# Softplus polynomial of a Mamba branch, from Horner steps to quadratic factors with ScalarE squares

## The reference

```python
x = x + _L0_attn_ref(_layernorm(x, axis=-1), ...)
x = x + _L0_xattn_ref(ctx_1024, _layernorm(x, axis=-1), ...)
x = x + _L0_ffn_ref(_layernorm(x, axis=-1), ...)

def _L0_xattn_ref(hidden_states, z, ...):
    ...
    x = silu(xc + conv_b[None, :, None])
    x_dbl = jnp.einsum('bdl,ed->bel', x, x_proj_w)
    dt_low, Bm, Cm = jnp.split(x_dbl, [dt_rank, dt_rank + d_state], axis=1)
    dt = jnp.einsum('brl,dr->bdl', dt_low, dt_proj_w)
    dt = jax.nn.softplus(dt + dt_proj_b[None, :, None])
    A = -jnp.exp(A_log)
    def step(state, inp):
        d, b, c, u = inp
        dA = jnp.exp(d[..., None] * A)
        state = state * dA + (d * u)[..., None] * b[:, None, :]
        y = jnp.einsum('bdn,bn->bd', state, c)
        return (state, y)
    ...
```

## Time and profile before

| | us |
|---|---|
| median of 3 runs | 1650.46 |
| lowest and highest | 1649.22, 1653.79 |
| the profiled execution, its own time | 1649.75 |
| the span that its trace covers | 1647.9 |
| PE busy | 1406.0 (85%) |
| VectorE busy | 1218.4 (74%) |
| ScalarE busy | 604.9 (37%) |

### The profile page before, as it was taken

One profiled execution on the slowest core, in us unless ns is written; L12 is line 12 of the kernel. 1 busy time (PEld: TensorE's weight loads), 2 busy tenths in 40 slices (PEclk: granted clock), 3 DMA queues, 4 the chain that ended last, 5 costly groups with the idle time before them and its releaser, 6 DMA issues.

```text
span 1647.9 us, 16148 instructions
## 1 busy us (share of the span) xinstructions
PE 1406.0 (85%) x5768; PEld 685.0 (42%) x5768; DVE 1218.4 (74%) x1411; ACT 604.9 (37%) x1436; POOL 111.9 (7%) x116
## 2 busy tenths in 40 slices
PE   5756767999888799899889699899879788799999
PEld 2333433443333354444334255444334345454434
DVE  4899996589989766759998865759998967623330
ACT  5165553323223584232232376242333267211110
POOL 0000001001100000000110000100210000100000
PEclk8855558999999699899999779899999869789999
DMA  4167761123666631112656822012556741101112
GB/s 185 39 147 153 154 141 27 44 66 108 143 141 166 166 66 26 39 50 78 159 128 159 196 68 52 26 37 84 124 131 152 173 135 27 26 13 64 48 32 83
DMA packets 53278, 158.81 MB, mean 96 GB/s; under 512 B 5072, under 2 KB 10704, under 8 KB 44752
## 3 DMA queue, kind: packets, MB, share of 16 engines
q0 software_dynamic: 9216, 67.11, 19.8%
q1 hardware_dynamic: 25664, 54.23, 9.9%
q10 hardware_dynamic: 18320, 36.45, 8.6%
HBM read 86.20 MB, written 4.46 MB: 55 GB/s over the span
## 4 chain that ended last, share of the span: by engine, by line
DVE 30%; issue 30%; PE 29%; DMA 6%; ACT 4%; POOL 2%; DVEq 0%; ACTq 0%; POOLq 0%
DVE state L1091 11%; DMA y_sb<-state 5%; PE ps_a L894 5%; DVE state L1086 4%; PE ps_a L974 4%; PE ps_a L820 3%; DVE state L1096 3%; PE ps_b L834 3%; PE ps_w L873 3%; PE ps_a L906 3%; POOL rstd L477 2%; PE ps_b L914 2%; PE ps_w L782 2%; ACT r L625 2%; DVE neg_max L1126 2%
## 5 line engine op out<-in xcount | busy, mean ns | idle before, releaser
L894 PE MATMUL ps_a<-xt,w_sb 128*128 128x512 f32 x704 | 319.2, 607 | 0.0
L1091 DVE TENSOR_TENSOR_SCAN state<-decay,state 128x2048 f32<-128x2048 f32 x64 | 282.8, 4418 | 5.3 <-ACT decay L583 0.5
L677 ACT ACTIVATE r<-ps_a 128x512 f32<-128x512 f32 x132 | 78.6, 596 | 380.6 <-PE ps_a L906 202.8
L894 PEld LDWEIGHTS ps_a<-xt,w_sb 128*128 128x128 f32 x704 | 138.1, 197 | 174.9 <-issue 174.9
L820 PE MATMUL ps_a<-r 32*128 32x512 f32 (+3 forms) x512 | 140.4, 634 | 81.7 <-ACT r L625 55.2
L906 PE MATMUL ps_a<-r,wb_sb 128*128 128x512 f32 x352 | 177.1, 628 | 35.9 <-DVE r L1267 33.7
L583 ACT ACTIVATE decay<-dt_sb,decay_rate 128x511 f32<-128x511 f32 x256 | 162.9, 712 | 104.9 <-DVE state L1096 72.2
L1260 DVE SCALAR_TENSOR_TENSOR r<-r,ps_a 128x512 f32<-128x512 f32 x132 | 89.9, 681 | 146.3 <-ACT r L677 146.3
L625 ACT ACTIVATE r<-ps_a,neg_max 128x128 f32<-128x128 f32 (+3 forms) x256 | 133.6, 534 | 116.6 <-DVE neg_max L1126 116.1
L974 PE MATMUL ps_a<-wd_sb,r 128*128 128x512 f32 x352 | 162.4, 613 | 0.0
L1086 DVE TENSOR_TENSOR state<-du_sb,bc_sb 128x2048 f32<-128x2048 f32 x64 | 146.3, 2286 | 4.7 <-DMA y_sb<-state 4.6
(11 more groups left out here) (120 smaller groups left out, 1475.7 us busy)
## 6 DMA issues: line engine op xcount, KB each, us to landing
y_sb<-state POOLq DMA_DIRECT2D x64, 1024.0 KB, 9.7
bc_sb<-bc_rows ACTq DMA_DIRECT2D x64, 512.0 KB, 5.1
w_sb<-in_w_tiles SPq DMA_DIRECT2D x44, 512.0 KB, 3.7
wd_sb<-in_w_down SPq DMA_DIRECT2D x44, 256.0 KB, 3.5
wb_sb<-in_w_adapt SPq DMA_DIRECT2D x44, 128.0 KB, 2.1
xa<-in_x SPq DMA_DIRECT2D x4, 1024.0 KB, 5.2
out_x<-xb SPq DMA_DIRECT2D x16, 256.0 KB, 7.0
xn_att<-in_ctx_t SPq DMA_DIRECT2D x4, 512.0 KB, 6.1
```

Source lines behind the costliest of these rows:

```text
L894: mm = nc.tensor.matmul(ps_a[:, 2 * (f % 2) + half, :], w_sb[:, slot, at + k * P:at + (k + 1) * P], xt[:, k, :], start=(k == 0), stop=Fals ...
L1091: nc.vector.tensor_tensor_scan(flat, decay[:, n % 2, :, :].rearrange("p j l -> p (j l)"), flat, 0.0, ALU.mult, ALU.add).then_inc(scan_chai ...
```

## The change

The polynomial is written by its roots. One root is real (and zero is another), the other eight form four pairs, each giving a quadratic factor (e + a)^2 + b. ScalarE computes the squares (e + a)^2 into `dt_sb`, which is free at this time, and VectorE multiplies the running product by (square + b). Both work on halves of 1024 elements. Poly pieces are now: one over 2048 for e*(e - line), eight over 1024, one over 2048 that multiplies by the leading coefficient and adds relu, and the product dt * u with its memset. There are 11 poly pieces where 12 stood, 8 of them half as long. ScalarE has 8 more instructions for each batch and loses its one-element copy. Squares 0 and 1 stand right behind softplus' inputs, and piece 0 waits for both. Square k waits for the piece that read the same half before it. The scan's pieces all move up by one place in the list while the numbers of pieces in the slots before attention stay; attention gets one piece fewer.

```diff
-POLY = log1p_coefficients(9)
-NPOLY = len(POLY)
+POLY_LINE, POLY_PAIRS = quadratic_factors(POLY)
+QUADS = 2 * len(POLY_PAIRS)
+NPOLY = QUADS + 3
...
-    pieces = [("poly", k) for k in range(NPOLY + 2)]
+    pieces = [("poly", k) for k in range(NPOLY)]
...
-        slots[between(at["poly", NPOLY + 1] if n < 2 else at["run", n - 2], at["run", n])]["decay"].append(n)
+        slots[between(at["poly", NPOLY - 1] if n < 2 else at["run", n - 2], at["run", n])]["decay"].append(n)
         slots[at["out", n]]["add"].append(n)
+    for k in range(2, QUADS):
+        free, used = at["poly", k - 1], at["poly", k + 1]
+        slots[between(free, used) if used > free else used]["square"].append(k)
...
-PIECES = NPOLY + 2 + 3 * NS
+PIECES = NPOLY + 3 * NS
...
-                    nc.scalar.activation(scrap_a[:], vec[0:1, 0:1], ACT.Copy).then_inc(softplus_in, 1)
+                    for k in range(2):
+                        square(b, k)
+
+            def square(b, k):
+                if k >= 2:
+                    act.wait_ge(poly_chain, b * NPOLY + k)
+                tiles = slice(k % 2 * JT // 2, (k % 2 + 1) * JT // 2)
+                nc.scalar.activation(square_sb[:, tiles, :], exp_v[:, tiles, :], ACT.Square,
+                                     bias=cst[:, C_ROOT + k // 2:C_ROOT + k // 2 + 1]).then_inc(square_ready, 1)
 
             def scan_inputs(b, slot):
+                for k in slot["square"]:
+                    square(b, k)
                 load_bc(b, slot)
                 make_decay(b, slot)
...
-                load_bc(0, PLAN_FIRST[DOWN + f])
                 project(0, f)
-                make_decay(0, PLAN_FIRST[DOWN + f])
+                scan_inputs(0, PLAN_FIRST[DOWN + f])
...
                     if n == 0:
-                        dve.wait_ge(softplus_in, b + 1)
-                        ts(du_sb[:], exp_v, POLY[-1], None, ALU.mult).then_inc(poly_chain, 1)
-                    elif n < NPOLY:
-                        dve.wait_ge(poly_chain, b * (NPOLY + 2) + n)
-                        stt(du_sb[:].rearrange("p j l -> p (j l)"), du_sb[:].rearrange("p j l -> p (j l)"),
-                            POLY[NPOLY - 1 - n], exp_v.rearrange("p j l -> p (j l)"), ALU.add, ALU.mult)\
-                            .then_inc(poly_chain, 1)
-                    elif n == NPOLY:
-                        dve.wait_ge(poly_chain, b * (NPOLY + 2) + n)
-                        tt(dt_sb[:], du_sb[:], relu_v, ALU.add).then_inc(poly_chain, 1)
+                        dve.wait_ge(square_ready, b * QUADS + 2)
+                        flat = exp_v.rearrange("p j l -> p (j l)")
+                        stt(whole, flat, -POLY_LINE, flat, ALU.add, ALU.mult).then_inc(poly_chain, 1)
+                    elif n <= QUADS:
+                        dve.wait_ge(square_ready, b * QUADS + n)
+                        dve.wait_ge(poly_chain, base + max(n - 2, 0) + 1)
+                        tiles = slice((n - 1) % 2 * JT // 2, ((n - 1) % 2 + 1) * JT // 2)
+                        part = du_sb[:, tiles, :].rearrange("p j l -> p (j l)")
+                        stt(part, square_sb[:, tiles, :].rearrange("p j l -> p (j l)"), POLY_PAIRS[(n - 1) // 2][1], part,
+                            ALU.add, ALU.mult).then_inc(poly_chain, 1)
+                    elif n == QUADS + 1:
+                        dve.wait_ge(poly_chain, base + n)
...
+                        stt(dt_sb[:].rearrange("p j l -> p (j l)"), whole, POLY[-1],
+                            relu_v.rearrange("p j l -> p (j l)"), ALU.mult, ALU.add).then_inc(poly_chain, 1)
```

More of the change, by code:

```diff
@@ L50, in log1p_coefficients, with quadratic_factors @@
     return [float(c) for c in fit.convert(kind=np.polynomial.Polynomial).coef]
+def quadratic_factors(coefficients):
+    import numpy as np
+    roots = np.roots(coefficients[::-1])
+    (line,) = [float(r.real) for r in roots if abs(r.imag) < 1e-9]
+    pairs = [(float(r.real), float(r.imag) ** 2) for r in roots if r.imag > 1e-9]
+    assert len(coefficients) == 2 + 2 * len(pairs)
+    return line, [pairs[k] for k in (1, 3, 0, 2)]
 POLY = log1p_coefficients(9)
-NPOLY = len(POLY)
+POLY_LINE, POLY_PAIRS = quadratic_factors(POLY)
+QUADS = 2 * len(POLY_PAIRS)
+NPOLY = QUADS + 3
 EVAL = [(0, 0)]
@@ L98, in plan @@
     assert sum(counts) == len(pieces), (sum(counts), len(pieces))
-    slots, at, k = [{"dve": [], "bc": [], "decay": [], "add": []} for _ in range(SLOTS)], {}, 0
+    slots, at, k = [{"dve": [], "bc": [], "decay": [], "add": [], "square": []} for _ in range(SLOTS)], {}, 0
     for s, count in enumerate(counts):
@@ L105, in plan @@
     for n in range(NS):
-        slots[between(at["poly", NPOLY - 4] if n < 2 else at["out", n - 2], at["mul", n])]["bc"].append(n)
-        slots[between(at["poly", NPOLY + 1] if n < 2 else at["run", n - 2], at["run", n])]["decay"].append(n)
+        slots[between(at["poly", NPOLY - 5] if n < 2 else at["out", n - 2], at["mul", n])]["bc"].append(n)
+        slots[between(at["poly", NPOLY - 1] if n < 2 else at["run", n - 2], at["run", n])]["decay"].append(n)
         slots[at["out", n]]["add"].append(n)
+    for k in range(2, QUADS):
+        free, used = at["poly", k - 1], at["poly", k + 1]
+        slots[between(free, used) if used > free else used]["square"].append(k)
     return slots
@@ L259, in decoder_layer @@
         xin_sb = relu_v
+        square_sb = dt_sb
         scrap = sb("scrap", [1, 1])
@@ L1352, in constant_table @@
     c[:, C_HALF:C_HALF + NT] = -0.5
+    c[:, C_ROOT:C_ROOT + len(POLY_PAIRS)] = [-re for re, _ in POLY_PAIRS]
     return c
```

15 lines of the change are left out of this document (10 added, 5 removed).

## The result

The changed kernel takes 1669.66 us (median of 4 runs, 1665.55 to 1672.66) against 1652.12 for the kernel before on the same chip (4 runs, 1649.22 to 1653.96). The ratio is 1.0106, with a 95% interval of 1.0078 to 1.0134: slower, by 13 to 22 us. The prediction said 1647, with 1641 to 1654.

The account below looks back on a forecast made before the run. VectorE was taken to bound batch 0's attention and PE the poly tiles, with the polynomial on the path in batch 0 alone. Batch 0's -7.8 plus +4.2 for batches 1 to 3 gave -3.6, so 1647, range 1641 to 1654.

Parts of the forecast that it names:

- attention of batches 1 to 3: Attention, batches 1 to 3: a scan leaves step 3, but PE waits only 0.33 there; -0.7 each, bounds 0 and -2.
- the durations: Polynomial pieces over 1024 elements: a ScalarE square takes 1.1 (bounds 1.05 and 1.38), a short VectorE product 1.22.
- batch 0: Batch 0: first rotation at 56.8, first scan at 77.2; 6.2 gained to the scan, 1.6 in attention, 7.8 in all.
- attention of batch 0: Batch 0's attention: short slots still cover the exponentials and waits for additions go, 1.6 gained; VectorE over 98% busy.
- rival 4: Batch 0's attention: uneven slots cost its gain, 15 pairs x 0.5 = 7.5, time 1654; 10%.
- the tiles: Feed-forward tiles, batches 1 to 3: 1.7 lost through decays ahead of a tanh, 0.7 regained; +1.0 for each batch.
- The 0.4 for squares ahead of tanhs: Poly tiles, batches 1 to 3: a square holds a tanh, so PE loses 0.4 at the base of tile 3.
- the second rotation: Down slots, batches 1 to 3: VectorE reaches it 2.2 earlier and waits 1.1 for PE's product, added to each batch.
- The wait at the first: Down slots, batches 1 to 3: 2.1 more VectorE work in down0 and down1 is hidden in its 5.34 wait for PE.
- Rival 3: Tiles, batches 1 to 3: tanhs behind squares and decays stop PE; up to +19, 1670, stated time 1656; 11%.
- Rival 1: Only batch 0 counts: held tanh and second rotation cost nothing; -12, 1638.5, or half, -8, stated time 1642.5; 24%.

Follow-up runs that it names:

- run 15: Not a follow-up run: the scan piece of n = 15 (2048 elements, 4.42) in attention of batches 1 to 3, in step 27 in the kernel before.
- run14_at_13: Changed kernel with its attention pieces of batches 1 to 3 at the earlier kernel's steps, except the scan of n = 14 at step 13: 1665.88 us, ratio 1.0085.
- before_two_runs_moved: Kernel before, with the scan of n = 14 moved from step 15 to 13 and that of n = 15 from 27 to 26: 1662.48 us, ratio 1.0063.
- the two kernels with early pieces: Changed kernel with five attention pieces in the first steps, 1633.56 us; and one with eight early-placed pieces and old tile and down-slot places, 1626.93.
- e15: Not a follow-up run: an evaluation slot in the feed-forward tiles, whose tanh on ScalarE stands behind the decays of n = 0 in the changed kernel.
- pieces_early: Changed kernel with its seven attention pieces of batches 1 to 3 at steps 1, 2, 3, 5, 7, 15, 19: 1633.56 us, ratio 0.9887.
- early_pieces_decay0_in_e16: pieces_early with the four decays of n = 0 of batches 1 to 3 put back behind the tanh they were moved ahead of: 1634.15 us, ratio 0.9886.
- new_poly_old_places: Changed kernel with an empty piece behind the last polynomial piece, so mul, run, out and decays keep the earlier kernel's slots: 1645.76 us, ratio 0.9970.

## Why the prediction was wrong, step by step

**The step that failed is the one on attention of batches 1 to 3**, "I take -0.7, bounds 0 and -2". It looked at one piece that left step 3 and at a wait of 0.33. It didn't look at the seven pieces that stay in the stage and are spread anew over its steps. This was in the order of the two kernels: run 14 from step 15 to 13, `mul` 15 from 23 to 22, run 15 from 27 to 26. The stage cost +6.0 in place of -0.7. It failed in a second way: the bounds were made from waits alone. A stop of 2.6 was priced nowhere at more than 2.6, where `run14_at_13` shows 18.6 in three batches, 6.2 each, and `before_two_runs_moved` 3.7 a batch for two moved scans. No term of the sum and no rival had the clock in it, and with the waits alone the range ended at 1654.

**Right: the durations.** A square was taken at 1.1 (bounds 1.05 and 1.38), a short product at 1.22 by the row of the maximum. Groups of the changed kernel by shape:

```profile
L1094 DVE SCALAR_TENSOR_TENSOR du_sb<-dt_sb,du_sb 128x1024 f32<-128x1024 f32 x32 | 38.2, 1220 | 5.1 <-ACT dt_sb L580 4.6
...
L580 ACT ACTIVATE dt_sb<-state,cst 128x1024 f32<-128x1024 f32 x32 | 35.8, 1144 | 5.6 <-DVE du_sb L1094 5.3
```

**Nearly right: batch 0.** Piece 0 started at 40.81 (41.05 predicted), but VectorE then waited 4.56 for square 4. That square stands behind ScalarE's copy of the first projection, which came at 50.82 and not at 47.7. So the first rotation came at 59.62, not 56.8. Here too the clock is what the sum had left out. It was at 0.50 from 40 to about 50, and the first 16 matmuls of the projections took 10.14 where they took 7.10 before (PE and windows, changed kernel, then the kernel before). That the squares bring this isn't shown: the clock is low at this place in every other trace too, those of the three further kernels with Horner steps among them, and only the kernel before was profiled without it:

```profile
44.08 10.14 PE L806 MATMUL ps_w<-xt,wq_sb 128*128 128x512 f32 x16 [0.73 <-ACT xt L614]
46.00:50.00 4.00, 4.00 (x6) 1.60 (x5) 2.01 (x2) 0.75 (x1) 0.00 (x0) 0.50 0.00 0
...
41.78 7.10 PE L782 MATMUL ps_w<-xt,wq_sb 128*128 128x512 f32 x16 [0.73 <-ACT xt L589]
46.00:50.00 4.00, 4.00 (x10) 1.63 (x9) 3.93 (x3) 0.86 (x2) 0.00 (x0) 1.00 0.54 172
```

Some of it came back in the ping-pong, since the wait for PE there was 2.58 in place of 3.62 and 0.64: run 0 started at 78.01 (77.2 predicted; 83.68 before). Timeline of VectorE:

```profile
40.81 2.29 DVE L1088 SCALAR_TENSOR_TENSOR du_sb<-state 128x2048 f32<-128x2048 f32 x1 [11.80 <-ACT dt_sb L580]
...
52.57 4.80 DVE L1094 SCALAR_TENSOR_TENSOR du_sb<-dt_sb,du_sb 128x1024 f32<-128x1024 f32 x4 [4.56 <-ACT dt_sb L580]
...
59.62 0.69 DVE L1138 TENSOR_TENSOR r<-r,cst 128x512 f32<-128x512 f32 x1
...
78.01 4.42 DVE L1124 TENSOR_TENSOR_SCAN state<-decay,state 128x2048 f32<-128x2048 f32 x1
```

The route came 6.3 earlier, of 7.8 predicted. One pair of executions doesn't measure this finely: in the nine profiled kernels with the changed batch 0 the route comes at 284.1 to 289.4 (287.8 in the middle), in the three with the old one at 293.3 to 297.2 (295.0), so the gain is nearer 7. (In the working, 6.5 less 0.4 is 6.1 and not 6.2.) In attention of batch 0 VectorE is busy for 29.90 of 30 in the window that had 28.97, so nothing is seen of waits in the short slot, and rival 4 is out:

```profile
150.00:180.00 30.00, 21.09 (x162) 13.19 (x162) 29.90 (x22) 17.66 (x49) 1.77 (x2) 0.56 0.71 154
```

**Right in size: the tiles.** The 0.4 for squares ahead of tanhs can't be seen: with the new polynomial in the old places the three stages sum to 775.7 against 776.0. For the new places I had +1.0 at the end of the tiles. Between the two kernels with early pieces, PE's first down product is 175.4, 175.3 and 175.2 behind the route against 174.3, 176.0 and 174.1, where the middle one started its first products at the lower clock: +1.1 between the other two. The evaluation of e16, against `base` of tile 1, is 1.4 later than in the kernel before (1.7 predicted): the tanh of e15 stands behind the decays of n = 0, and VectorE waits 1.51 for it where it waited 0.31. Putting these decays back into e16 frees that tanh, but now run 0 waits 0.80 for them, and `mul` 0 is still one place ahead. So e16 gained 1.2 and the last tile's start only 0.3. The test had moved the wait rather than taken it away (VectorE, batch 1, `pieces_early`, then `early_pieces_decay0_in_e16`):

```profile
373.41 0.69 DVE L1293 SCALAR_TENSOR_TENSOR r<-r,ps_a 128x512 f32<-128x512 f32 x1 [1.51 <-ACT r L702]
...
378.00 4.43 DVE L1124 TENSOR_TENSOR_SCAN state<-decay,state 128x2048 f32<-128x2048 f32 x1 [0.80 <-ACT decay L608]
```

**Right: the second rotation.** A wait of 1.1 was predicted for PE's product at the second rotation, and it is 1.11. The wait at the first was to shrink by the 2.1 by which the list is ahead; it shrank by 3.3, from 5.34 to 2.01. The changed kernel, to be read against the earlier trace rows:

```profile
481.54 0.69 DVE L1141 TENSOR_TENSOR r<-ps_w,cst 128x512 f32<-128x512 f32 x1 [2.01 <-PE ps_w L813]
...
489.27 0.69 DVE L1141 TENSOR_TENSOR r<-ps_w,cst 128x512 f32<-128x512 f32 x1 [1.11 <-PE ps_w L813]
```

What I had not seen in the down slots is that PE now also waits for ScalarE, in each of the three batches, which it didn't before:

```profile
510.08 1.16 PE L813 MATMUL ps_w<-r,cst 128*128 128x512 f32 x2 [1.97 <-ACT r L630]
```

Together the places cost 3.0 for each batch (8.9 / 3), of 2.1 predicted.

**The rivals.** Rival 3, at its far end, gave 1670 (its stated time was 1656), and the time came out at 1669.7, but not by its mechanism: it needed squares and decays to hold PE in the tiles, and with the new polynomial alone the tiles are as they were. That the two numbers meet is chance. The rule of the Trainium skill beside it, that plain arithmetic belongs on VectorE (ScalarE: Activation LUTs, Rules for kernel authors), isn't borne out here either, in fp32 (the page gives its reason for bf16): a square of 1024 elements takes 1.14 on ScalarE and the short product 1.22 on VectorE, and the polynomial alone is 0.3% faster. Rival 1 had the second rotation and the held tanh cost nothing; but both cost about what was predicted. (Its -8 is not half of -12 but the middle between -12 and the forecast's -3.6.) `new_poly_old_places` comes near its time (1645.76; 1642.5), but without those places, so this doesn't speak for it.

## What to carry to other kernels

A change that takes one item out of a list which a rule spreads over slots moves every item behind it: compare the orders stage by stage, and price the moved items before the new arithmetic. Where PE is nearly full and its clock is high, a wait of it is to be priced at the clock that it may cost behind it (here 3.7 to 6.2 a stage in the mean where a stop of 2.6 was brought in, 0.7 to 10.5 in single stages), not at its length. Long VectorE pieces belong where PE has the most queued, or where its clock is low anyway; ahead of, or between, two wide maxima on which it waits they brought the stops here.
